# Cross attention's score maxima lag by three steps; two DMA queue orders and the scan's soft-plus are rearranged

## The reference

```
x = _layernorm(x + _L0_attn_ref(x, ...))                 # delta rule attention
x = _layernorm(x + _L0_xattn_ref(ctx_1024, x, ...))      # selective scan
x = _layernorm(x + _L0_ffn_ref(x, ...))                  # FFN with sign weights
x = _layernorm(x + _L1_attn_ref(x, ...))                 # local, landmark and global attention
x = _layernorm(x + _L1_xattn_ref(x, ctx_1024, fside, fside, ...))   # cross attention
x = _layernorm(x + _L1_ffn_ref(x, ...))                  # FFN with ternary weights
```

```
dt = softplus(einsum('brl,dr->bdl', dt_low, dt_proj_w) + dt_proj_b)
state = state * exp(d * A) + (d * u) * b;   y = sum over n of state * c
```

```
q = rope(x @ Wq);  k = rope(ctx @ Wk);  v = ctx @ Wv
w = softmax(q @ k.T / sqrt(16));        out = (w @ v) @ Wout + bout
```

## Time and profile before

| | us |
|---|---|
| median of 3 runs (3025.77 to 3038.11) | 3027.39 |
| the profiled execution, its own time | 3033.01 |
| its span, first to last instruction | 3031.2 |
| TensorE busy in the span | 2622.0 (86%) |
| VectorE busy | 1899.5 (63%) |
| ScalarE busy | 1466.8 (48%) |
| GpSimd busy | 1153.8 (38%) |

### The profile page before, as it was taken

One profiled execution on the slowest core, in us unless ns is written; L12 is line 12 of the kernel. 1 busy time (PEld: TensorE's weight loads), 2 busy tenths in 40 slices (PEclk: granted clock), 3 DMA queues, 4 the chain that ended last, 5 costly groups with the idle time before them and its releaser, 6 DMA issues.

```text
span 3031.2 us, 50557 instructions
## 1 busy us (share of the span) xinstructions
PE 2622.0 (86%) x20138; PEld 1425.8 (47%) x20154; DVE 1899.5 (63%) x2978; ACT 1466.8 (48%) x2612; POOL 1153.8 (38%) x1072
## 2 busy tenths in 40 slices
PE   7899999887787866899989898888779999999787
PEld 5666666542232322788545454444433343333244
DVE  4343434438999999566266656657546666676477
ACT  4352535226666653244253543626226666666355
POOL 0555455517777766000244435162233333331000
PEclk9898999997898978999989899899879999999889
DMA  3313131412313230333243313344074445451301
GB/s 95 92 57 99 57 99 57 103 57 90 132 35 112 71 112 14 153 109 146 89 122 115 106 67 105 99 124 163 15 158 107 106 106 121 105 108 48 127 29 42
DMA packets 196766, 284.50 MB, mean 94 GB/s; under 512 B 84388, under 2 KB 86468, under 8 KB 195636
## 3 DMA queue, kind: packets, MB, share of 16 engines
q1 hardware_dynamic: 196532, 281.27, 31.8%
HBM read 192.08 MB, written 63.31 MB: 84 GB/s over the span
## 4 chain that ended last, share of the span: by engine, by line
PE 43%; DVE 10%; issue 4%; ACT 3%; DMA 2%; POOL 2%; SPq 1%; DVEq 0%; ACTq 0%; POOLq 0%
PE ps L236 8%; PE ps L3645 4%; PE ps L3658 4%; PE ps L2085 4%; PE ps L2096 4%; PE ps L3577 3%; PE ps L3594 2%; PE ps L3628 2%; PE ps L2751 1%; PE ps L2759 1%; PE ps L3582 1%; DVE arena L3014 1%; DVE arena L3012 1%; PE ps L2809 1%; ACT cross L3738 1%
## 5 line engine op out<-in xcount | busy, mean ns | idle before, releaser
L236 PE MATMUL ps<-arena 128*128 128x512 f32 (+3 forms) x1248 | 453.6, 515 | 14.9 <-ACT arena L2851 6.1
L3830 DVE TENSOR_REDUCE cross<-ps 128x1 f32<-128x512 f32 x512 | 327.8, 686 | 175.3 <-PE ps L3628 175.2
L1721 POOL TENSOR_TENSOR arena<-arena 128x1024 f32<-128x1024 f32 x128 | 305.9, 2394 | 120.8 <-DVE arena L1713 120.6
L3738 ACT ACTIVATE cross<-ps 128x512 f32<-128x512 f32 x512 | 276.7, 593 | 154.4 <-PE ps L3645 154.2
L1737 PE MATMUL ps<-arena 128*128 128x512 f32 x512 | 267.8, 665 | 39.1 <-POOL arena L1721 39.1
L1713 DVE TENSOR_TENSOR_SCAN arena<-ps,arena 128x1024 f32<-128x1024 f32 x128 | 291.6, 2279 | 9.2 <-ACT ps L1704 9.1
L236 PEld LDWEIGHTS ps<-arena 128*128 128x128 f32 (+2 forms) x1264 | 184.8, 152 | 235.4 <-issue 163.5
L1704 ACT ACTIVATE ps<-arena 128x511 f32<-128x511 f32 x256 | 164.9, 679 | 156.5 <-DVE arena L1713 156.2
L609 POOL TENSOR_TENSOR arena<-arena 128x31 f32<-128x31 f32 (+15 forms) x217 | 135.4, 624 | 200.4 <-DMA arena<-d_a 183.9
L1737 PEld LDWEIGHTS ps<-arena 128*128 128x128 f32 x512 | 105.5, 215 | 192.9 <-issue 124.8
L3645 PE MATMUL ps<-cross,cross 50*128 50x512 f32 x512 | 156.4, 506 | 31.7 <-ACT cross L3738 22.8
(11 more groups left out here) (364 smaller groups left out, 5167.8 us busy)
## 6 DMA issues: line engine op xcount, KB each, us to landing
arena<-d_bc SPq DMA_DIRECT2D x32, 1024.0 KB, 5.5
cross<-d_parts SPq DMA_DIRECT2D x192, 128.0 KB, 4.6
arena<-d_x SPq DMA_DIRECT2D x16, 1024.0 KB, 5.4
d_parts<-cross SPq DMA_DIRECT2D x32, 512.0 KB, 3.6
d_x<-arena SPq DMA_DIRECT2D x48, 256.0 KB, 2.5
arena<-in_D_wlm SPq DMA_DIRECT2D x12, 1024.0 KB, 6.3
...
```

The source lines that it names most:

```text
L236: ins = pe.e.matmul(ps[:m, :n], lhsT(k), rhs(k), start=(k == 0), stop=(k == chunks - 1))
L1721: pool.e.tensor_tensor(h, h, s.bc[turn % s.SLOTS][:, 1], ALU.mult).then_inc(*pool.up("scan_hC"))
L3738: act.e.activation(s.E[:, k % 2, j], s.rexp.bank((u, i)), ACT.Exp).then_inc(*s.rexp.empty(act, (u, i)))
L3830: dve.e.tensor_reduce(s.mx[:, u % 2, t, h:h + 1], s.rmax.bank((u, m)), AX.X, ALU.max, negate=True).then_inc(*s.rmax.empty(dve, (u, m)))
```

## The change

In the scan, input projection 0 moves from turn 4 to 7, and the soft-plus of chunks 2 and 3 moves by one or two turns. In the landmark stage the load of batch 1's x moves from local step -2 to step 1 of batch 0, so behind three pairs of swaps. In cross attention the maxima of a unit lie three steps later (`LATER = 3`: steps 3 to 15 of iteration u-1 and 0 to 2 of iteration u), "mT" moves from steps 8 and 1 to 11 and 4, "Rq" from 3, 3, 5, 5 to 5, 5, 6, 6, "aT" from 6 to 7, "Rk" from 7 to 8. At the start of the stage SyncE unfolds unit 0 before it swaps unit 1, issues the two copies of unit 0's maxima ahead of an unfolding, and loads the output weights last.

```diff
-    PE_IN = {4: (0, None), 8: (1, 0), 9: (1, 1), 10: (2, 0), 11: (2, 1), 12: (3, 0), 13: (3, 1)}
+    PE_IN = {7: (0, None), 8: (1, 0), 9: (1, 1), 10: (2, 0), 11: (2, 1), 12: (3, 0), 13: (3, 1)}
...
-    OWN_SOFT = {"raw": {0: [2], 2: [3]}, "abs": {2: [2], 4: [3]}, "ln": {8: [2, 3]}, "floor": {3: [2], 5: [3]},
-                "log": {9: [2], 10: [3]}, "dt": {10: [2], 11: [3]}}
+    OWN_SOFT = {"raw": {0: [2], 4: [3]}, "abs": {2: [2], 6: [3]}, "ln": {9: [2, 3]}, "floor": {3: [2], 7: [3]},
+                "log": {10: [2], 11: [3]}, "dt": {11: [2], 12: [3]}}
...
-            if phase == "local" and k == -2 and b == 0:
+            if phase == "local" and k == 1 and b == 0:
                 sp.e.wait_ge(*s.ring.at_filled(sp, ("xT", 0, T - 1)))
                 s.sp_x(sp, 1)
...
+    LATER = 3
...
+    def max_step(self, i, step):
+
+        u, at = divmod(self.PAIRS * (i + 1) + step - self.LATER, self.PAIRS)
+        return self.unit(u), at
+
     def small(self, i):
...
-        if s.unit(i) is not None:
-            items.append((("mT", i, 1), [1]))
         if s.unit(i - 1) is not None:
             items.append((("turn", i - 1, 1), [2]))
+        if s.unit(i) is not None:
+            items.append((("mT", i, 1), [1 + s.LATER]))
         if s.unit(f) is not None and i != -1:
-            items.append((("Rq", f), [3, 3, 5, 5]))
+            items.append((("Rq", f), [5, 5, 6, 6]))
         if s.unit(i - 1) is not None:
-            items.append((("aT", i - 1), [6]))
+            items.append((("aT", i - 1), [7]))
         if f > 0 and s.unit(f) is not None and i != -1:
-            items.append((("Rk", f), [7, 7]))
-        if s.unit(i + 1) is not None:
-            items.append((("mT", i + 1, 0), [8]))
+            items.append((("Rk", f), [8, 8]))
         if s.unit(f) is not None:
             items.append((("V", f), [9, 9]))
         if s.unit(i) is not None:
             items.append((("turn", i, 0), [10]))
+        if s.unit(i + 1) is not None:
+            items.append((("mT", i + 1, 0), [8 + s.LATER]))
...
+        for w in (1, 0):
+            s.sp_unfold(sp, 0, w)
         for w in range(2):
             s.sp_swap(sp, 1, w)
-        for w in (1, 0):
-            s.sp_unfold(sp, 0, w)
-        s.sp_late(sp)
         for f in range(1, s.AHEAD):
             for w in range(2):
                 if f + 1 < s.AHEAD:
                     s.sp_swap(sp, f + 1, w)
-                s.sp_stack(sp, f, w)
-                if f + 1 == s.AHEAD and w == 0:
+                s.sp_keep(sp, f, w)
+                if (f, w) == (1, 1):
                     s.sp_rows(sp, 0, 0)
+                if (f, w) == (s.AHEAD - 1, 1):
+                    s.sp_rows(sp, 0, 1)
+                s.sp_unfold(sp, f, w)
+        s.sp_late(sp)
...
-                if s.unit(i + 1) is not None:
-                    for m in tiles:
-                        s.pe_max(pe, i + 1, m)
+                u, at = s.max_step(i, step)
+                if u is not None:
+                    for m in (2 * at, 2 * at + 1):
+                        s.pe_max(pe, u, m)
```

10 lines of the change are left out of this document (5 added, 5 removed).

## The result

The changed kernel takes 3047.3 us against 3029.0 (medians of 8 runs each), a ratio of 1.0059 (95% interval 1.0037 to 1.0080): 17.9 us slower, where 7.8 was forecast. The time lies inside the range, on the side to which the forecast pointed. In the prediction's own terms a ratio above 1.005 is "slower", to which it gave a chance of 0.25, and 0.63 to "same". That the sum is off by only 10 us is partly luck: cross attention was set 14 us too low (+15.4 against +29.6) and the gain in the scan 8 us too low (-5 against -12.8), and the two errors have opposite signs. The profiled execution has a span of 3050.3, 19.1 above that of before.

The account below looks back on a forecast made before the run. TensorE's list, with a pause in bare odd steps, was taken to bound cross units, VectorE the scan. Cross +15.4, scan -5 and landmark -2.6 sum to +7.8 on the profiled 3033.0 us; on the median 3035, range 3014 to 3050.

Parts of the forecast that it names:

- Bare odd steps: Cross attention: a bare odd step costs 1.00 us, side work there is free up to 1.00; +1.94 a unit, nine units 17.5.
- Rival 2: Cross attention: the pause is not filled by side work, so placement is free; 3011 us, chance 0.12.
- The late copy: Cross units 1, 2, 3, 12: the next unit's maxima copy, behind the query unfolding, lands late; +2.55 each, 10.2 together.
- These units take 35.3: Cross units 1, 2, 3 and 12, without output projection, last until the maxima copy lands at 35.3 us, +2.55 each.
- Don't wait: Cross units with output projection take 36.55 us, longer than the copy chain's 35.3, so don't wait for it.
- Rival 4: Cross units: more TensorE pauses make the clock fall, up to 5.5 us a unit, 82 for 15; 3117 us, chance 0.02.
- The output weights: Cross start: their load, 3.1 us, now ahead of x and unit 3's swap, is covered by unit 0; 0, to +4.
- The start: Cross start: maxima copy issued earlier, first exponential tile at 2253 instead of 2266.28; -13.3 us, bounds -3.6 and -17.
- The scan: Scan: with "abs" at turn 6, batches 0 and 3 give back VectorE's wait; -5 us, bounds 0 and -9.
- The landmark: Landmark stage: later x load lets projection 5's swap land earlier, shortening GpSimd's and TensorE's waits; -2.6 us, bounds 0 and -4.
- Unit 15: Last cross unit, which had no maxima, gets three pairs of them at 0.33 each; +1.0 us.
- Unit 13: Cross unit without projections: "mT" leaving a free step costs 0.53, "aT" entering one gains as much; 0.

Follow-up runs that it names:

- e4: The kernel before with only the projections' new places ("Rq", "aT", "Rk"), maxima not lagging: ratio 1.0108, 3065.0 us.
- e7: The changed kernel with the copy of the next unit's first maxima issued ahead of the unfolding of the projected queries: ratio 1.0017, 3034.7 us.
- e8: e7 with side work put in odd steps ("Rq" in 1 and 3, "aT" in 5, "Rk" in 7): ratio 0.9910, 2999.8 us.
- e1: The kernel before with the scan's part of the change alone: ratio 0.9958, 3015.6 us.
- e2: The kernel before with only the later load of batch 1's x in the landmark stage: ratio 1.0002, 3027.0 us.
- e3: The kernel before with only SyncE's new order at the start of cross attention, maxima not lagging: ratio 0.9973, 3020.5 us.
- e6: The kernel before with the scan's part and SyncE's order at the start of cross, without lag or new places: ratio 0.9951, 3012.5 us.
- e5: The changed kernel with the old places of the projections, all else as changed: ratio 0.9995, 3025.3 us.

## Why the prediction was right, and where it was not

**Bare odd steps.** Right. The forecast of +1.94 for units with output projection came out as 2.0 to 2.3 in units 6, 7, 10 and 11, and 2.8 in units 5 and 9, where VectorE was late as well for the turning of the maxima in step 11 (3.9 us instead of 3.1). Rival 2, that placement is free, is refuted by e4 and by the 32 us between e7 and e8.

**The late copy.** The mechanism was right: "These units take 35.3" gave 34.1, 35.3 and 37.7 for units 1, 2 and 3, and the same +2.55 on unit 12, 37.2, gave 39.6. "Don't wait" held too: none of units 4 to 11 ends with a wait for the copy.

**The clock.** This is the step that failed. Rival 4 took the clock as all or nothing, with a chance of 0.02, and the sum has no term for it. The short pauses that it feared did nothing: with pauses of 0.45 in steps 2 and 4, units 5 to 7 and 9 to 11 ran at 1.00. But the clock fell behind longer pauses, among them the waits of 1.80, 2.51 and 1.43 for the copy. Counted from the windows (a unit's length, times what its clock lacks to 1, times two), the 16 units of the changed kernel spent 58 us at the lower level, those of the kernel before 25, and those of e1, e2, e3 and e6 24 to 32. At half the clock 26 to 34 us more cost at most 13 to 17, an estimate that takes TensorE as busy throughout; the forecast lacks 13.2. Not all of this is the change: the falls in units 4 (behind ScalarE) and 12 are there in e1, e2 and e6 too. e7 shows that a good part hangs on the copy: with the copy first the waits are gone, the units spend 44 us at the lower level instead of 58, and the kernel gains 12.7.

**The output weights.** "I count 0, to +4" holds for the changed kernel, as far as waits tell. GpSimd waits 8.49 for unit 3's swap, but TensorE waits for no transfer within unit 0 and 0.79 for the copy at its end. Unit 0 grows by 6.4 where 1.94 was forecast because TensorE is busy for 5.1 us more at 0.74 instead of 0.81 of the clock. The term was too low in other kernels with the same order: TensorE waits 8.3 us for late transfers in e5 and 4.5 in e8.

**The start.** Right: 12.3 for 13.3, of it 9.1 from SyncE's order (e3) and the rest, by the difference of e5 and e6, from the tiles that the lag takes away. What I named as the last link was wrong: not the copy but the tiles for the maxima ended last.

**The scan.** Right in place, too low by more than half: 11 to 13 for 5. The forecast let batches 1 and 2 come out at zero, setting 1.4 of cost against the wait; the cost did not come. And it counted waits alone: 8.2 of the gain are waits at the recurrence, 2.9 are waits at the drive, and 1.7 lie in the durations of other operations, which GpSimd can stretch (last section).

**The landmark.** Both waits shrank by 4.5 to 5.1, more than 2.6, part of it only moved, and 2.2 is left at the end of the stage, as far as fourteen executions can tell.

Unit 15 was forecast at +1.0 and came out 1.1 shorter. Its 28.5 before held a stretch at the lower clock (0.94 in the unit); e1, e2 and e6 take 27.1 at 1.00, and against these it grew by 0.3. Unit 13, forecast at 0, grew by 1.5 with the wait for the copy and its clock. A copy that lands after 2 us would, by the prediction's own +2.55 against +1.41 for four units, have made the sum 4.6 lower, not 4.7.
